# Two groups of heads in flight in a chain of four cross-attentions on one core

## The reference

```
x0 = x + mha(norm(x), norm(ctx))              # 8 heads of 32
u  = (norm(x0) @ W_in.T + b_in) @ Bmat        # one row per token
s_t = silu(s_{t-1} @ A.T) + u_t               # scan over the 1024 tokens
x1 = x0 + s @ Cmat + mod[batch]
x2 = x1 + attention(norm(x1), norm(ctx))      # 16 heads of 64, causal
y  = x2 + attention(x2, ctx), masked; x3 = norm(y)        # 16 heads of 16, sum + 1e-9
x4 = x3 + attention(norm(x3), norm(ctx2)), masked         # 16 heads of 16
out = x4 + gelu(norm(x4) @ fc1 + b) @ fc2 + b
```

## Time and profile before

| | before |
|---|---|
| runs, us | 1370.93, 1373.24, 1376.13 |
| profiled execution: span, us | 1373.0 |
| PE busy | 1333.4 (97%) |
| DVE busy | 903.9 (66%) |
| ACT busy | 674.3 (49%) |
| POOL busy | 558.9 (41%) |

### The profile page before, as it was taken

The page is one execution under the profiler, slowest core; times in us unless marked ns, Lnnn a source line. Parts: engine busy times, 40 slices in busy tenths (PEclk is TensorE's granted clock), DMA queues, the critical chain, the costliest instruction groups (busy, mean ns, idle before and its releaser), DMA issues.

```text
span 1373.0 us, 23019 instructions
## 1 busy us (share of the span) xinstructions
PE 1333.4 (97%) x8771; PEld 1124.9 (82%) x8771; DVE 903.9 (66%) x2204; ACT 674.3 (49%) x1495; POOL 558.9 (41%) x700
## 2 busy tenths in 40 slices
PE   7999999999999999999999999999999999899999
PEld 5989987787888788878888888779877987688778
DVE  4778872776756766676576556784768467746771
ACT  4657766134554444544545435445344543464454
POOL 4465431107513643364346211572156216621661
PEclk9999999999999999999999999999999999999999
DMA  4334402200000000000000001000000000000000
GB/s 112 77 112 130 132 21 81 64 8 1 1 16 16 1 13 5 17 0 9 1 9 1 24 5 29 0 1 16 16 1 1 17 16 1 1 5 12 1 1 16
DMA packets 48463, 34.10 MB, mean 25 GB/s; under 512 B 22177, under 2 KB 45536, under 8 KB 48352
## 3 DMA queue, kind: packets, MB, share of 16 engines
q1 hardware_dynamic: 48304, 32.59, 8.5%
q10 hardware_dynamic: 48, 0.01, 0.0%
HBM read 23.26 MB, written 8.39 MB: 23 GB/s over the span
## 4 chain that ended last, share of the span: by engine, by line
PE 84%; DVE 6%; POOL 5%; SPq 2%; ACT 2%; issue 1%; DMA 1%; DVEq 0%; POOLq 0%; ACTq 0%
PE ps L886 11%; PE ps L876 10%; PE ps L836 10%; PE ps L932 8%; PE ps L943 8%; PE ps L855 8%; PE ps L846 6%; PE ps L896 5%; PE ps L802 5%; PE ps L785 4%; PE ps L1037 2%; SPq L611 1%; PE ps L1050 1%; POOL pr L1603 1%; POOL pr L1617 1%
## 5 line engine op out<-in xcount | busy, mean ns | idle before, releaser
L1578 POOL TENSOR_TENSOR rstd<-mv,halfneg 128x1 f32<-128x1 f32 x192 | 109.1, 570 | 340.7 <-DVE mv L1313 338.7
L1617 POOL TENSOR_TENSOR pr<-mx,pr 128x616 f32<-128x616 f32 x128 | 155.9, 1220 | 215.3 <-DVE mx L1347 213.9
L1158 ACT ACTIVATE pr<-pr 128x616 f32<-128x616 f32 x224 | 159.7, 715 | 145.9 <-POOL pr L1617 74.5
L1162 ACT ACTIVATE pr<-ps 128x512 f32<-128x512 f32 x224 | 132.7, 596 | 162.9 <-PE ps L855 162.7
L886 PEld LDWEIGHTS ps<-vtab,pr 128*128 128x128 f32 (+1 forms) x1280 | 153.0, 191 | 14.1 <-ACT pr L1162 10.5
L886 PE MATMUL ps<-vtab,pr 128*128 128x102 f32 (+1 forms) x1280 | 161.9, 275 | 2.0 <-ACT pr L1162 0.9
L855 PE MATMUL ps<-ident,pr 128*128 128x128 f32 (+1 forms) x1120 | 159.4, 275 | 3.5 <-POOL pr L1603 2.7
L1137 ACT ACTIVATE tt<-ps 128x256 f32<-128x256 f32 x160 | 60.9, 383 | 183.5 <-PE ps L785 183.4
L855 PEld LDWEIGHTS ps<-ident,pr 128*128 128x128 f32 (+1 forms) x1120 | 125.5, 139 | 30.1 <-POOL pr L1603 9.1
L876 PE MATMUL ps<-vwo,pr 128*128 128x256 f32 (+1 forms) x640 | 148.9, 381 | 0.0
L1411 DVE TENSOR_TENSOR xt<-xt,ps 128x256 f32<-128x256 f32 x192 | 79.7, 416 | 101.8 <-PE ps L896 50.4
(11 more groups left out here) (200 smaller groups left out, 2368.8 us busy)
## 6 DMA issues: line engine op xcount, KB each, us to landing
out_dram<-xt SPq DMA_DIRECT2D x64, 128.0 KB, 1.7
xt<-in_x_dram SPq DMA_DIRECT2D x32, 128.0 KB, 2.2
xt<-out_dram SPq DMA_DIRECT2D x32, 128.0 KB, 2.1
fc<-in_L_xattn_fc_w_dram SPq DMA_DIRECT2D x2, 1024.0 KB, 6.8
wk<-in_L_xattn_wkv_dram SPq DMA_DIRECT2D x4, 512.0 KB, 5.0
front<-in_L_xattn_wkv_dram SPq DMA_DIRECT2D x4, 512.0 KB, 5.9
wo<-in_L_xattn_wo_dram SPq DMA_DIRECT2D x1, 1024.0 KB, 5.2
kb<-in_L_xattn_wq_dram SPq DMA_DIRECT2D x1, 1024.0 KB, 6.8
```

The lines of the kernel that those rows point to most:

```text
L1158: ac(v, v, ACT.Exp, scale=-ATTN[key[0]].scale).then_inc(done["expo"], 1)
L1162: ac(pr[:, run.lane, 0:4 * P], bank(run.lane, 0), ACT.Copy).then_inc(done["pturn_main"], 1)
L1617: p.tensor_tensor(p8, mx[:, run.lane, :].unsqueeze(2).to_broadcast([P, HG, KEYS]), p8, ALU.subtract).then_inc(done["below"], 1)
```

## The change

In the second, third and fourth attention both groups of heads of a tile are now in flight. The scores of group 1 wait only until DVE has read group 0's out of the banks (`shift`, `bound`) and no longer for group 0's `resid` or `heads`. Group 1's probabilities have a buffer of their own, `pr2`, in a part of `front`. `mx` and `rec` hold both groups. The transposes of group 1 follow those of group 0. One `mix` works both groups off (the second attention sums both in one bank, the third and fourth use a bank for each), and there is one `den_eps`, one `recip` and one `heads` for both in the third and fourth, and one `resid` in the second. PE issues the same 8771 matmuls; DVE has 1975 steps where it had 2167.

To make room in `front`, the temporary values of the tables move from `front` and a buffer of their own to `modrow` (which `v_sb` may write only after the last `keep`), and the buffer of the second pair's weights in `front` is halved: its parts 2 and 3 are loaded when the keys are made. The very first `shift` of group 1 waits for the last `vwo_mm` of the first pair. `laid` of the first attention is two semaphores. All five strings of `TURNS` are new, for both passes and the tables.

```diff
 def attention_steps(a):
+    if a is L0:
+        steps = [("query", "0"), ("query_bias", "0")]
+        steps += [(s, "0.0") for s in ("scores", "rowmax", "shift", "expo", "pturn", "pturn_main", "pturn_rest", "mix", "recip", "heads")]
+        return steps + [("turn", "0o"), ("turned", "0o"), ("proj", "0"), ("resid", "0")]
+    first, second = f"{a.name}.0", f"{a.name}.1"
+    top = ["scores", "rowmax", "shift"] if a is L1 else ["scores", "bound", "rowmax", "below"]
+    masked = ["maskmul"] if a is L2 else []
+    norm = ["rowsum", "recip", "weigh"] if a is L1 else []
+    turns = ["pturn", "pturn_main", "pturn_rest"]
     steps = [] if a is L1 else [("query", a.name), ("query_bias", a.name)]
-    for g in range(a.groups):
-        k = f"{a.name}.{g}"
-        steps += [("scores", k)]
-        steps += [("bound", k), ("rowmax", k), ("below", k)] if a in (L2, L3) else [("rowmax", k), ("shift", k)]
-        steps += [("expo", k)]
-        if a is L2:
-            steps += [("maskmul", k)]
-        if a is L1:
-            steps += [("rowsum", k), ("recip", k), ("weigh", k)]
-        steps += [("pturn", k), ("pturn_main", k), ("pturn_rest", k), ("mix", k)]
-        if a is L1:
-            steps += [("resid", k)]
-        else:
-            if a is L2:
-                steps += [("den_eps", k)]
-            steps += [("recip", k), ("heads", k)]
+    steps += [(s, first) for s in top] + [("expo", first)] + [(s, second) for s in top]
+    steps += [(s, first) for s in masked + norm] + [("expo", second)] + [(s, first) for s in turns]
+    steps += [(s, second) for s in masked + norm + turns] + [("mix", a.name)]
     if a is not L1:
-        o = a.name + "o"
-        steps += [("turn", o), ("turned", o), ("proj", a.name), ("resid", a.name)]
-    return steps
+        steps += [("den_eps", a.name)] * (a is L2) + [("recip", a.name), ("heads", a.name)]
+        steps += [("turn", a.name + "o"), ("turned", a.name + "o"), ("proj", a.name)]
+    return steps + [("resid", a.name)]
...
-        "1023a0123aaaaa01aa0a1aaaaaaa2aaaa2303101a2230031aa1aa2a23300a1a12aa2aa30aa03a1a1a2aa2303011223301200a01312213323"
-        "bbbbaa00112233001122330123000111bb223332001122330011223302130213"),
+        "aa2aaaa203aaaaa30aaa11aaaaaaa2120103aaaa3aa21aa13a2a3aa00aaa231312aa10230132a3321201030230121203002a3101013301aa"
+        "2b21203b0121220313030b1b213220033b13021b110023323000212331113022"),
...
-        vtmp = {"2": front[0:KEYS, 4096:4096 + PAIR * H].rearrange("p (b n) -> p b n", b=PAIR), "3": sb("vtmp3", [KEYS, PAIR, H])[:, :, :]}
+        vtmp = {"2": modrow[0:KEYS, 0:PAIR, :], "3": modrow[0:KEYS, PAIR:2 * PAIR, :]}
...
+        pr2 = front[:, 2048:2048 + LANES * 5 * P].rearrange("p (l n) -> p l n", l=LANES)
...
-        mx = sb("mx", [P, LANES, HG])
-        rec = sb("rec", [P, LANES, HG])
+        mx = sb("mx", [P, LANES, 2, HG])
+        rec = sb("rec", [P, LANES, 2, HG])
...
-                front[:, 0:4096].rearrange("p (k n) -> p k n", k=KC)]
+                front[:, 0:2048].rearrange("p (k n) -> p k n", k=KC)]
...
-        laid = {n: sem("laid" + n) for n in "023"}
+        laid = {n: sem("laid" + n) for n in ("00", "01", "2", "3")}
...
+        def group(key):
+            return int(key[2])
+
+        def probs(key, lane):
+            return (pr2 if group(key) else pr)[:, lane, :]
+
+        def heads_view(key, lane):
+            return probs(key, lane)[:, 0:HG * KEYS].rearrange("p (h n) -> p h n", n=KEYS)
+
+        def each_head(small, key, lane):
+            return small[:, lane, group(key), :].unsqueeze(2).to_broadcast([P, HG, KEYS])
...
-                    sp.wait_ge(laid["0"], 2 * LAY * 16)
-                else:
+                    sp.wait_ge(laid["00"], LAY * 16)
+                    sp.wait_ge(laid["01"], LAY * 16)
+                elif part < WKV_PARTS // 2:
                     sp.wait_ge(done["vwo_mm"], at("vwo_mm", f"0{L1.groups - 1}{PAIR - 1}{TILES - 1}"))
-                sp.dma_start(wkv1[pair][:, :, cols], by_rows("L1_xattn_wkv")[:, :, cols]).then_inc(wkv1_in, 16)
+                else:
+                    sp.wait_ge(done["k_mm"], at("k_mm", f"11{L1.chunks - 1}"))
+                to = slice(cols.start % L1.width, cols.start % L1.width + n) if pair else cols
+                sp.dma_start(wkv1[pair][:, :, to], by_rows("L1_xattn_wkv")[:, :, cols]).then_inc(wkv1_in, 16)
...
-                lay_values(sp, L0, vtmp0[:, two, :], vtab["0"][:, two, :, :, :], laid["0"])
+                lay_values(sp, L0, vtmp0[:, two, :], vtab["0"][:, two, :, :, :], laid[f"0{key}"])
...
-                    sp.wait_ge(done["mix"], max(at("mix", f"{a.name}.1", r) for r in last_runs(1, 0)))
+                    sp.wait_ge(done["mix"], max(at("mix", a.name, r) for r in last_runs(1, 0)))
...
-                    pe.wait_ge(done["resid"], at("resid", "1.0", run))
-                else:
-                    pe.wait_ge(done["heads"], at("heads", f"{a.name}.0", run))
+                    pe.wait_ge(done["shift"], at("shift", "1.0", run))
+                else:
+                    pe.wait_ge(done["bound"], at("bound", f"{a.name}.0", run))
...
                 s = {"1": "weigh", "2": "maskmul"}.get(key[0], "expo")
                 pe.wait_ge(done[s], at(s, key, run))
+                if group(key):
+                    pe.wait_ge(done["pturn_main"], at("pturn_main", f"{a.name}.0", run))
+                    pe.wait_ge(done["pturn_rest"], at("pturn_rest", f"{a.name}.0", run))
+                elif a is not L0:
+                    s = "shift" if a is L1 else "bound"
+                    pe.wait_ge(done[s], at(s, f"{a.name}.1", run))
                 for j in range(TILES):
                     last = turn_in(bank(lane, j // 4)[0:TROWS[j], j % 4 * P:(j % 4 + 1) * P],
-                                   pr[:, lane, j * P:j * P + TROWS[j]], ident[:, :])
+                                   probs(key, lane)[:, j * P:j * P + TROWS[j]], ident[:, :])
                 last.then_inc(done["pturn"], 1)
...
-                pe.wait_ge(done["pturn_main"], at("pturn_main", key, run))
-                pe.wait_ge(done["pturn_rest"], at("pturn_rest", key, run))
+                for k in [key] if a is L0 else [f"{key}.{g}" for g in range(a.groups)]:
+                    pe.wait_ge(done["pturn_main"], at("pturn_main", k, run))
+                    pe.wait_ge(done["pturn_rest"], at("pturn_rest", k, run))
...
+                for g in range(a.groups):
+                    pt = [probs(f"{a.name}.{g}", lane)[0:TROWS[j], j * P:(j + 1) * P] for j in range(TILES)]
+                    for j in range(TILES):
+                        if a is L1:
+                            last = mm(o[:, 0:H], pt[j], vwo[0:TROWS[j], b, g, j, :], start=g == j == 0,
+                                      stop=g == a.groups - 1 and j == TILES - 1)
...
+                if pair and g == 0 and c == 0:
+                    pe.wait_ge(wkv1_in, 16 * 2 * WKV_PARTS)
+                w = (0 if pair else L1.width) + (g * GC + c) * P
...
+                if key == "1.1" and run.no == RUNS:
+                    dve.wait_ge(done["vwo_mm"], at("vwo_mm", f"0{L1.groups - 1}{PAIR - 1}{TILES - 1}"))
...
+                v.tensor_scalar(mx[:, run.lane, :, :], heads_out(key, run.lane)[:, :, :, L2.hd], 1e-9, None, ALU.add)\
...
-                w = HG * a.hd
-                v.tensor_tensor(z[:, lane, g * w:(g + 1) * w].rearrange("p (h d) -> p h d", d=a.hd),
-                                mixed(key, lane)[:, :, 0:a.hd],
-                                rec[:, lane, :].unsqueeze(2).to_broadcast([P, HG, a.hd]), ALU.mult).then_inc(done["heads"], 1)
+                v.tensor_tensor(z[:, lane, 0:H].rearrange("p (g h d) -> p g h d", g=a.groups, d=a.hd),
+                                heads_out(key, lane)[:, :, :, 0:a.hd],
+                                rec[:, lane, 0:a.groups, :].unsqueeze(3).to_broadcast([P, a.groups, HG, a.hd]), ALU.mult).then_inc(done["heads"], 1)
...
-                if key[0] == "1":
-                    dve.wait_ge(done["mix"], at("mix", key, run))
-                    src = bank(lane, 0)
-                    if key[2] == "0":
-                        dve.wait_ge(done["prebias"], at("prebias", "1", run))
-                    else:
-                        dve.wait_ge(done["resid"], at("resid", "1.0", run))
-                else:
-                    dve.wait_ge(done["prebias"], at("prebias", key, run))
-                    s, k = ("fc2", "mb") if key == "m" else ("proj", key)
-                    dve.wait_ge(done[s], at(s, k, run))
-                    src = bank(lane, 0 if key == "m" else 1)
+                dve.wait_ge(done["prebias"], at("prebias", key, run))
+                s, k = {"1": ("mix", "1"), "m": ("fc2", "mb")}.get(key, ("proj", key))
+                dve.wait_ge(done[s], at(s, k, run))
+                src = bank(lane, 0 if key in "1m" else 1)
...
+                    dve.wait_ge(done["keep"], counts.total["keep"])
```

(20 more changed lines are left out.)

158 lines of the change are left out of this document (74 added, 84 removed).

## The result

The changed kernel takes 1415.22 us (median of 4 runs, 1414.38 to 1416.16) against 1372.14: ratio 1.0308 (1.0292 to 1.0324), slower. The forecast was slower too, but at 1387 (1360 to 1406): 28 us too low, and outside the range. (1372.14 is the median of the kernel before over four runs, one more than stood ahead of the prediction.)

The account below looks back on a forecast made before the run. PE, busy 97% of the span, was taken to bound the kernel, so only its gaps could change. 1373.0 - 24 (groups) + 17 (second pass) + 8 (switch) + 10 (first pass) + 3 (clock) = 1387 us, range 1360 to 1406.

Parts of the forecast that it names:

- Start of the second pass: Lane 2's get of run 8 stands behind 24 small DMAs in SP's queue; PE stalls 16.7 us, taken as +17.
- Switch to the second pair: Lane 1's get of run 12 stands behind one v_lay of 10.15 us; PE stalls +8 us, bounds 0 and 12.
- Masks in the first pass: At the first pass's start POOL waits for the masks' DMA; PE loses 13 us, net +10, bounds -2 and +16.
- late `load`: In the first pass, the load of run 1 behind the 13 weights in SP's order adds 3 us.
- Both groups in flight: Second pass: a lane offers PE the second group's scores while the first is elsewhere; -24 us, bounds +5 and -57.
- start-to-start excess of 57 us: PE from 320 on: matmuls' time beyond their usual step, read as gaps; 40 us the most any order brings.
- The listed waits: PE's visible waits from 320 on: nine kinds, 18.4 us in all, none longer than 1.8 us.
- not by more than half: Sign: the prediction is wrong if PE's idle time from 320 on doesn't fall by more than half.
- VectorE: 42 us less: Merged steps take 42 us off DVE, busy 66%; off PE's path, this is worth nothing by itself.
- Clock: PE's granted clock falls after long stalls: three cost +5 us, one was there before, net +3.
- (b): Rival: the stalls come and the groups bring nothing, with POOL and DVE setting the pace; 1411 us, chance 0.10.

Follow-up runs that it names:

- e1: The changed kernel with three gets (lane 2 runs 8 and 9, lane 1 run 12) issued ahead of the v_lay DMAs in SP's order; 1390.78 us.
- e8: e4 with the three mask instructions on POOL moved behind the last step of the first pass; 1361.75 us, ratio 0.9921.
- e11: e1 with the masks also moved behind the first pass, the changed order of the first pass otherwise kept; 1375.13 us, ratio 1.0015.
- e12: e11 with SP's loads of run 1 issued ahead of the 13 weights, as before the change; 1377.78 us, ratio 1.0032.
- e4: The changed kernel with the first pass in the old order on all engines and the three gets issued early; 1366.36 us, ratio 0.9950.
- e14: The kernel before with bound, rowmax, below and maskmul of the third and fourth attention cut to one head of eight; 1360.09 us, ratio 0.9903.
- e7: e4 with a DVE addition of 128x256 put ahead of den_eps and every recip of the third and fourth attention; 1403.17 us, ratio 1.0216.
- e9: e4 with 96 additional DVE reductions behind heads of the third (two) and fourth (one) attention; 1380.66 us, ratio 1.0044.
- e15: e4 with heads of the third and fourth attention cut to one head of eight in each group; 1361.74 us, ratio 0.9918.
- e16: The kernel before with both groups' heads of the third and fourth attention cut to one head of eight; 1371.45 us, ratio 0.9989.
- e3: The changed kernel with the first pass in the order of before on all five engines, the second pass as changed; 1392.20 us, ratio 1.0135.
- e5: e4 with maskmul on POOL cut to one head of eight in the third attention; 1363.56 us, ratio 0.9931.
- e6: The kernel before with maskmul on POOL cut to one head of eight in the third attention; 1371.64 us, ratio 0.9988.

## Why the prediction was wrong

*Start of the second pass: right.* A stall of 16.7 was forecast; PE's wait is 14.4 us. The 24 issues took 20.4 us where 21.0 were reckoned, and PE had 10.2 us of work ahead where 8.6 were. The chain was the one written down: `get` behind 24 small DMAs, `resume`, `shift`, scores.

*Switch to the second pair: right.* +8 forecast, 8.14 measured. With the half clock behind them the two come to 24.4 us (e1); forecast 25, and some 3 of clock.

*Masks in the first pass: the stall right, the net partly by luck.* A stall of 13 was forecast and the wait is 11.5 us; the net of both places is 11.1 (e8, e11), forecast +10. But the +10 contains 3 for the late `load`, which was wrong: with the loads first the kernel is 2.6 us slower (e12). Without them and with a stall's share of the clock the term was 9.

*Step that was missing: the rest of the new order of the first pass.* Nothing was put down for it, since I looked for long waits in SP's and POOL's order alone. It costs 13.4 us (e11 against e8). Which engine's order makes it was not separated; the small waits name ACT's copies, norms and `resid`.

*Step that failed: "Both groups in flight", -24.* It is -7.0 (e4: 0.9934 to 0.9966). I took a start-to-start excess of 57 us for waits that a better order could close. The excess, added up in one way for three traces (for each matmul from 264 us on, what the time to the next one's start exceeds the median of its line and shape), is 125 us before, 116 in e4 and 111 in e14, where most of the element work of two attentions is gone. So most of it is no waiting for that work, and that work in all is worth 13.9 us (e14). The listed waits, 19.5 us from 320 on in twelve kinds (the forecast counted nine, 18.4), would have set a closer bound; but e4 still has 17.6 there, in other kinds, and PE's idle time from 320 on fell from 25.2 to 22.0 us, not by more than half.

The second half of this step was VectorE: 42 us less, and worth nothing by themselves. Both parts failed. The steps that were merged take 38.6 us less in e4, close to the forecast, but the page shows VectorE busy for 882.5 us there and 903.9 before, 21.4 less (17.5 in the changed kernel). 11.4 us of the difference went to the norms, the same 192 instructions in either kernel; the largest of their three rows, before and in e4:

```profile
L1322 DVE TENSOR_SCALAR zt<-xt,mv,rstd 128x256 f32<-128x256 f32 x128 | 60.8, 475 | 29.5 <-POOL rstd L1578 27.4
```

```profile
L1343 DVE TENSOR_SCALAR zt<-xt,mv,rstd 128x256 f32<-128x256 f32 x128 | 69.5, 545 | 26.2 <-POOL rstd L1590 24.3
```

Their median is 0.41 us in both; 20 of them are held up by a running POOL instruction before and 45 in e4 (last section). That VectorE's time is worth something is shown by e7 and e9, where it costs when it grows, and e15 and e16, where 1 us less gives 0.17 to 0.31. By this price 21.4 us are worth 4 to 7 (an estimate), so that most or all of the 7.0 can come from the fewer steps and little from the second group in flight. No run separates the two: the kernel before with merged steps, or two groups in flight with the old steps, was not tried. The chain behind the last mix did not shrink at all: one `heads` of 0.42 us and one `recip` of 0.25 stand where the second group's 0.29 and 0.20 stood. That a written order keeps PE's next step where it was is my reading of the difference between lengthening and shortening; no run isolates it.

*Clock: too small.* +5 was forecast for three stalls and +3 net. Behind the three stalls PE is busy for 17.0 us at the lower level, which costs 8.5; the kernel before has two spells of 3.4 us, which cost 3.4. The net is 5. The granted clock is down in and behind the stalls and nowhere else in between, and the terms measured by differences contain it.

*Sum.* 1373 - 7.0 + 24.4 + 11.1 + 13.4 = 1414.9. These terms are differences between the runs, so their sum must meet the 1415.2 measured and proves nothing; the test that they add up is e4, 1366.4, against 1367.8 from e1 and e3. Against the forecast of 1387, 17 us come from the groups, 13.4 from the first pass's order and 1 from the masks; the two stalls with all of the clock were 4 too high. Of the rivals, (b) had nearly the time (1411) for the wrong reason, by luck: its price stood on groups that bring nothing and POOL's pace, where the groups bring 7, 66 us of `maskmul` are worth 2 or 3 (e5, e6), and what filled the gap is the first pass's order, which no rival had.

## What to carry to other kernels

Before a `get`, count the issue time of what stands ahead of it in the queue of the engine that issues it: a dozen tiny DMAs held SP for 10 us, longer than any wait of PE in the kernel before. The three stalls came out at 14.4, 8.1 and 11.5 us where 16.7, 8 and 13 were worked out from the order and the durations; the value of overlap was missed by a factor of three, and a run with the work cut away bounds it. Busy time saved on an engine isn't the sum of the steps that go: here 11 of 39 us went to longer waits for another engine. A new order should be taken over one stage at a time: the second pass's was worth having, the first pass's was not. With three DMA issues and the masks moved and the first pass left in its old order, the same two groups in flight make a kernel that is 0.8% faster than before (e8), a third of it from the masks; with the new order of the first pass kept it is 0.15% slower (e11).
